# Attention scores as one fp32 product instead of three fp32r products, ten transpositions of the probabilities instead of twelve, and new orders on every engine

## The reference

```python
q = (einsum('bld,ed->ble', layernorm(x), Wq) + bq)      # 16 heads of 8
k, v = split(einsum('bmc,ec->bme', ctx, Wkv) + bkv)
att = softmax(einsum('blhd,bmhd->blmh', q, k) * scale, axis=2)
x = x + tanh(g_xattn) * (einsum('blmh,bmhd->blhd', att, v) @ Wo.T + bo)
cur = layernorm(x)
for r in range(4):                                       # 4 rounds, 4 experts, top 2
    cw = softmax over the two best of (cur @ Wg[r] + bg[r])
    cur = cur + sum_e cw[e] * (gelu(cur @ W1[e] + b1[e]) @ W2[e] + b2[e])
x = x + tanh(g_ffn) * cur
```

## Time and profile before

| | |
|---|---|
| median of 3 runs | 482.22 us (480.55 to 482.83) |
| the profiled execution | 479.67 us, of which its span, first to last instruction, is 477.9 us |
| busy in the span: TensorE, weight loads | 459.7 us (96%), 371.5 us (78%) |
| VectorE, ScalarE, GpSimd | 372.4 us (78%), 380.4 us (80%), 75.4 us (16%) |
| granted TensorE clock, mean | 0.995 of full speed |

### The profile page before, as it was taken

How to read it: one execution, slowest core, us unless ns; L and a number is a source line. 1 busy time by engine, 2 the same in 40 slices (tenths; PEclk the granted TensorE clock), 3 DMA queues, 4 the chain that set the end, 5 groups by cost and what they waited for, 6 DMA issues and landing times.

```text
span 477.9 us, 9057 instructions
## 1 busy us (share of the span) xinstructions
PE 459.7 (96%) x2969; PEld 371.5 (78%) x2969; DVE 372.4 (78%) x749; ACT 380.4 (80%) x781; POOL 75.4 (16%) x116
## 2 busy tenths in 40 slices
PE   6788999999999999999999999999999999999997
PEld 5566778878888788888888888888888888888885
DVE  4789889889796968876877787779767876887776
ACT  2587898878695987887888698869887988798773
POOL 4484898432200000000000000000000000000000
PEclk9899999999999999999999999999999999999999
DMA  5490000022002200300040004000400030023001
GB/s 138 132 253 15 1 17 16 2 91 89 2 0 90 86 3 1 139 40 1 1 178 1 1 1 178 0 2 2 176 1 0 23 158 1 1 78 123 22 2 45
DMA packets 15173, 25.21 MB, mean 53 GB/s; under 512 B 3505, under 2 KB 11542, under 8 KB 13078
## 3 DMA queue, kind: packets, MB, share of 16 engines
q1 hardware_dynamic: 11152, 22.05, 13.1%
q0 software_dynamic: 2592, 2.10, 2.6%
q10 hardware_dynamic: 1382, 0.49, 0.4%
HBM read 22.82 MB, written 1.18 MB: 50 GB/s over the span
## 4 chain that ended last, share of the span: by engine, by line
PE 86%; DVE 6%; ACT 3%; issue 3%; DMA 1%; SPq 1%; DVEq 0%; ACTq 0%
PE ps L1420 12%; PE ps L1407 12%; PE ps L1422 12%; PE ps L1421 12%; PE ps L1409 12%; PE ps L1408 12%; PE ps L1299 2%; PE ps L1318 2%; PE ps L1323 2%; PE ps L1284 1%; DMA gates<-in_g_ffn_dram 1%; DVE rT_sb L942 1%; ACT prob L716 1%; DVE least L918 1%; ACT probT L725 1%
## 5 line engine op out<-in xcount | busy, mean ns | idle before, releaser
L977 DVE TENSOR_TENSOR h_lo<-g_sb,h_hi 128x512 fp32r<-128x512 f32 x256 | 170.0, 688 | 75.6 <-ACT h_hi L829 75.4
L822 ACT ACTIVATE g_sb<-ps,cols 128x512 f32<-128x512 f32 x256 | 174.7, 694 | 35.6 <-PE ps L1409 34.1
L829 ACT ACTIVATE h_hi<-g_sb 128x512 fp32r<-128x512 f32 x256 | 156.0, 641 | 0.0
L1420 PE MATMUL ps<-h_hi,w_hi 128*128 128x512 f32 x252 | 101.6, 403 | 0.0
L1407 PE MATMUL ps<-x_hi,w_hi 128*128 128x512 f32 x256 | 101.1, 395 | 0.0
L1409 PE MATMUL ps<-x_hi,w_lo 128*128 128x512 f32 x256 | 100.1, 391 | 0.0
L1408 PE MATMUL ps<-x_lo,w_hi 128*128 128x512 f32 x256 | 99.8, 390 | 0.0
L1422 PE MATMUL ps<-h_hi,w_lo 128*128 128x512 f32 x252 | 99.6, 395 | 0.0
L1421 PE MATMUL ps<-h_lo,w_hi 128*128 128x512 f32 x252 | 99.5, 395 | 0.0
L1409 PEld LDWEIGHTS ps<-x_hi,w_lo 128*128 128x128 f32 x256 | 48.0, 188 | 11.3
L1408 PEld LDWEIGHTS ps<-x_lo,w_hi 128*128 128x128 f32 x256 | 48.1, 188 | 10.8
(11 more groups left out here) (153 smaller groups left out, 470.9 us busy)
## 6 DMA issues: line engine op xcount, KB each, us to landing
cwb_even<-cw_rows SPq DMA_DIRECT2D x8, 1024.0 KB, 5.3
cwb_odd<-cw_rows SPq DMA_DIRECT2D x8, 1024.0 KB, 4.9
w_hi<-in_L_ffn_W_dram POOLq DMA_DIRECT2D x2, 1024.0 KB, 8.2
x_sb<-in_x_dram SPq DMA_DIRECT2D x4, 256.0 KB, 5.9
w_in<-in_L_ffn_W_dram SPq DMA_DIRECT2D x1, 1024.0 KB, 6.0
out_dram<-xn SPq DMA_DIRECT2D x3, 256.0 KB, 2.3
ctx_sb<-in_ctx_dram ACTq DMA_DIRECT2D x4, 115.5 KB
v_st<-v_sb SPq DMA_DIRECT2D x8, 38.5 KB
```

The lines of the kernel that those rows point to most:

```text
L822: nc.scalar.activation(g_sb[:, k, :], ps[:, k, :], ACT.Gelu_apprx_tanh, bias=b1_c[:, e * NF + k:e * NF + k + 1]).then_inc(gelu_done, 1)
L829: nc.scalar.activation(h_hi[:, u % 2, k, :], g_sb[:, k, :], ACT.Copy).then_inc(hi_done, 1)
L977: nc.vector.tensor_tensor(h_lo[:, u % 2, k, :], g_sb[:, k, :], h_hi[:, u % 2, k, :].bitcast(F32), ALU.subtract).then_inc(lo_done, 1)
L1420: mm(yb, w2_hi[:, w], hh, start=k == 0, stop=False)
```

## The change

1. **Scores.** `q_hi`, `q_lo`, `k_hi`, `k_lo` and all work that splits q and k are gone. `scores` multiplies `q_st` by `k_st`, both fp32, one matmul for each head group.
2. **Blocks.** Two head groups (616 rows of probabilities) are now cut together into five blocks of 128, 128, 128, 128 and 104 rows, ten blocks a batch. The transposition groups hold 4, 4 and 2 blocks (`GROUPS`). `v_st` and `row_head` get a further index z for the group's place in its pair, and the list `pieces` gets as long as there are cuts.
3. **Orders.** Other orders in the start (input transfers, transpositions, warm-up matmuls, the tanh of the gates) and in the slots (tables and the order inside a slot, on all engines).

```diff
+    for z in range(NZ):
+        for j in range(HQ):
+            at, end = (HQ * z + j) * M, (HQ * z + j + 1) * M
...
+                pieces.append((z, j, k - 2 * z, at - P * k, stop - P * k, at - first, stop - first))
...
-            passes = ((q_hi, k_hi), (q_hi, k_lo), (q_lo, k_hi))
...
-                for n, (qs, ks) in enumerate(passes):
-                    for q in range(NQ):
-                        rows = slice(32 * q, 32 * q + 32)
-                        t = mm(ps[:, SC + q, 0:HM], qs[rows, c % 2, at], ks[rows, b % 2, :],
-                               start=n == 0, stop=n == len(passes) - 1)
+                for q in range(NQ):
+                    rows = slice(32 * q, 32 * q + 32)
+                    t = mm(ps[:, SC + q, 0:HM], q_st[rows, c % 2, at], k_st[rows, b % 2, :], start=True, stop=True)
                 t.then_inc(scores_done, 1)
...
-                for k in range(PG):
-                    q, c = (PG * g + k) // KC, (PG * g + k) % KC
-                    n, at = rows_of[c], q * HM + RP * c
-                    t = tr(bank(key)[0:n, k * L:(k + 1) * L], prob[:, b % 2, at:at + n], ident[:, :])
+                for k in range(GROUPS[g], GROUPS[g + 1]):
+                    n, at = rows_of[k % BLOCKS], k // BLOCKS * HP + k % BLOCKS * P
...
-        CTX_AT = {4: 2, 6: 3}
-        K_AT = {1: 1, 4: 2, 8: 3}
+        CTX_AT = {2: 2, 7: 3}
+        K_AT = {0: 1, 4: 2, 8: 3}
         V_AT = {3: 1, 7: 2, 10: 3}
-        LK_AT = {2: 1, 6: 2, 10: 3}
...
-        LOW_AT = {2: 1, 5: 2, 9: 3}
         W_LAG = 1
-        PT_DVE = {0: 2, 6: 1}
+        GROUPS = (0, 4, 8, 10)
+        PT_DVE = {2: 0}
...
-                for j, k, row, row_end, m, m_end in pieces:
-                    sp.dma_start(v_st[row:row_end, c % 2, k, DH * j:DH * (j + 1), :],
-                                 v_sb[m:m_end, c, DH * j:DH * (j + 1), :]).then_inc(v_ld[c], 16)
+                for z, j, k, row, row_end, m, m_end in pieces:
+                    sp.dma_start(v_st[row:row_end, c % 2, k, z, DH * j:DH * (j + 1), :],
+                                 v_sb[m:m_end, c, z, DH * j:DH * (j + 1), :]).then_inc(v_ld[c], 16)
...
-            act.wait_ge(gates_ld, 32)
-            nc.scalar.activation(tgates[:, :], gates[:, :], ACT.Tanh).then_inc(tg_ready, 1)
             move_k(0)
...
+            exponentials(0, 1)
+            stage_q("b")
             act.wait_ge(gates_ld, 32)
             nc.scalar.activation(tgates[:, :], gates[:, :], ACT.Tanh).then_inc(tg_ready, 1)
```

More of the change, by code:

```diff
@@ L59, in flamingo_gated_block @@
     KC = 3
-    RP = -(-HM // KC)
-    rows_of = [min(RP, HM - RP * c) for c in range(KC)]
-    pieces = []
[L63 to L71, removed]
+    NZ = 2
+    PAIRS = NQ // NZ
+    HP = NZ * HM
+    BLOCKS = -(-HP // P)
+    rows_of = [min(P, HP - P * k) for k in range(BLOCKS)]
+    assert BLOCKS == 5 and HM <= P * KC
+    pieces = []
+    for z in range(NZ):
+        for j in range(HQ):
+            at, end = (HQ * z + j) * M, (HQ * z + j + 1) * M
+            first = at
+            while at < end:
+                k = at // P
+                stop = min(end, P * (k + 1))
+                assert 0 <= k - 2 * z < KC
+                pieces.append((z, j, k - 2 * z, at - P * k, stop - P * k, at - first, stop - first))
+                at = stop
     with ExitStack() as stack:
@@ L160, in flamingo_gated_block @@
         kT = early("kT", [P, B * M])
[L161 to L164, removed]
+        q_st = early("q_st", [P, 2, CH])
         shifted = early("shifted", [P, 2, HM])
-        k_hi = early("k_hi", [P, 2, HM], F32R)
-        k_lo = early("k_lo", [P, 2, HM], F32R)
+        k_st = early("k_st", [P, 2, HM])
         prob = early("prob", [P, 2, NQ * HM])
@@ new lines, in expert_order @@
+            def expert_order():
+                nc.gpsimd.memset(lgs[:, :, :], 0.0).then_inc(zero_done, 1)
+                nc.gpsimd.memset(wg_w[:, :, :, :].bitcast(F32), 0.0).then_inc(zero_done, 1)
+                nc.gpsimd.memset(before[:, :, :], 1.0).then_inc(order_step, 1)
+                nc.gpsimd.memset(after[:, :, :], 1.0).then_inc(order_step, 1)
+                pool.wait_ge(order_step, 2)
+                nc.gpsimd.affine_select(out=before[:, :, :], in_=before[:, :, :], compare_op=ALU.is_ge, fill=0.0,
+                                        base=-1, pattern=[[1, E], [-1, E]], channel_multiplier=0).then_inc(order_ready, 1)
+                nc.gpsimd.affine_select(out=after[:, :, :], in_=after[:, :, :], compare_op=ALU.is_ge, fill=0.0,
+                                        base=-1, pattern=[[-1, E], [1, E]], channel_multiplier=0).then_inc(order_ready, 1)
@@ L700, in stage_q @@
                     act.wait_ge(scores_done, TC * (c - 1))
-                nc.scalar.activation(q_hi[:, g, at], bank(("Q", c))[:, at], ACT.Identity,
-                                     bias=bq_s[:, 0:1]).then_inc(q_hi_done, 1)
+                nc.scalar.activation(q_st[:, g, at], bank(("Q", c))[:, at], ACT.Identity,
+                                     bias=bq_s[:, 0:1]).then_inc(job_act, 1)
             def exponentials(b, half):
@@ L1133, in _ @@
                     smallest(b + 1, 1)
+                if b >= 3:
+                    add_residual(b - 3)
                 if b + 1 < B:
                     smallest(b + 1, 0)
+                if b == WEIGHTS0_SLOT:
+                    weights(0)
+                if b in PT_DVE:
+                    copy_pt(b, PT_DVE[b])
+                if b in MOMENTS:
+                    moments(*MOMENTS[b])
+                if b + 1 < B:
+                    shift(b + 1)
+                if b == ROUTER0_SLOT:
+                    router(0)
+                if b in NORMALISE:
+                    normalise(NORMALISE[b])
+                if b == ROUTER1_SLOT:
+                    router(1)
+                if b in SPLIT_X:
+                    split_x(SPLIT_X[b])
                 if b == 3:
```

325 lines of the change are left out of this document (143 added, 182 removed).

## The result

| | before | after |
|---|---|---|
| median of 6 runs | 481.51 us (479.74 to 482.83) | 475.69 us (474.77 to 478.36) |
| the profiled execution | 479.67 us, span 477.9 us | 478.16 us, span 476.4 us, clock 0.992 |

The ratio of after to before is 0.9902, 95% interval 0.9875 to 0.9929, which is 4.7 us less (3.4 to 6.0). Ratios here leave out four executions far above the others of their kernel, one each of before_fp32 and v_early_experts_later and two of before_twelve_pieces. Three of after's executions took 474.8 to 475.0 us at a granted clock of 1.000, three took 476.4 to 478.4 us at 0.992 to 0.996; the profile is of the second kind. A second profile of the same kernel (the last experiment) is of the first kind, 475.00 us with a span of 473.3 us.

What follows compares the result with a forecast made beforehand. The expert stage was taken as fixed, TensorE-bound, and loop slots as set by a circle through three engines. Start -1.7, slots -1.7, -0.1 and -1.45, late values +2.1 and +0.2 gave -2.65 us: median 479.6 us, range 474.5 to 485.

Steps and rivals of the forecast that it cites:

- A: Whole kernel, as summed: late values give back half of the gain; -1 to -4.5 us; chance 0.42.
- B: Whole kernel: values not late, or the loop packs better; 472 to 477.6 us; chance 0.26.
- Scores: Score product on TensorE: four fp32 row tiles overlap, 0.52 us in all, +0.12 us a batch.
- Rival D: Score product: fp32 row tiles don't overlap, 6 to 12.5 us on top, 486 to 492 us; chance 0.13.
- By the rule the scores would cost a third more: Score product: the skill's four passes for true fp32 against three fp32r passes, a third more cost.
- Values: SyncE's twelve pieces take 9.4 us, values there 10.2 to 10.6 us after the copy; stalls +2.1 and +0.2 us.
- Slots with q: Slots 2, 5, 9: VectorE's q_lo and its wait fall out; sum -1.7 us.
- Slots 3 and 4: Router's weights move behind everything: slot 3 6.83 to 5.2, slot 4 5.08 to 6.6 us; sum -0.1 us.
- But VectorE then begins slot 4 2.6 us late: Slot 4: the router's weights delay VectorE's start by 2.6 us, so the slot takes 6.6 us, from 5.08.
- Slot 5: Slot 5: 5.91 to 5.1 us without q_lo; values' lead 10.2 us, a stall of 0 to 0.35, taken as 0.2.
- The start: Before the second scores: tanh moves behind, splits of k and q go; second scores near 18.2 us, -1.7 us.
- Slots 10 to 15: End of the loop: only a little transposition work is lost; -0.5 us.

Runs made afterwards that it cites:

- before_fp32: The kernel before with q and k in fp32, one product and no low parts or splits; blocks and orders as before: 479.13 us, ratio 0.996.
- v_early_experts_later: v_early with GpSimd's two 1 MB expert-weight transfers one slot later and the splitting of these weights in slots 5 to 12: ratio 0.9877.
- before_twelve_pieces: The kernel before with each of the six transfers that place the values issued as two, each with half of the columns: ratio 1.0024.
- the last experiment: The changed kernel run once more without any edit, for a profile at full clock: 475.00 us.
- twelve_blocks: The changed kernel with twelve blocks of 102 or 103 rows and six value transfers again; fp32 scores and new orders stay: 474.03 us, ratio 0.987.
- three_pass: The changed kernel with the fp32 score product replaced by three fp32r passes over the high parts, low parts left out: 477.39 us, ratio 0.9922.
- before_twelve_pieces_again: The kernel before with its six value transfers issued as twelve, run once more for a profile at full clock: 479.58 us.
- v_early: The changed kernel with the values made in slots 1, 6 and 10 in place of 3, 7 and 10: 473.73 us, ratio 0.9855.
- v_early_one_warm: v_early with one warm-up product instead of six ahead of the first scores: 475.59 us, ratio 0.9881.
- router_weights_slot6: The changed kernel with the split of the router's weights in slot 6 in place of slot 3: 476.26 us, one run.
- experts_wait: v_early_one_warm with GpSimd issuing the 1 MB w2_hi transfer only once all twelve pieces of the first values have landed: 475.64 us, ratio 0.9879.

## Why the prediction was right, and where not

The forecast was 479.6 us and -2.65 us; measured were 475.69 us and about -4.7 us by the ratio. The sign and the range hold; the size is 2 us off. Of the rivals, A's mechanism came true, values that are late and give back part of the gain, but not its number: -4.7 us is more than its -4.5, and 475.69 us lies outside its 477.7 to 481.2 and inside B's 472 to 477.6. B's first half, values that are not late, is false; its second, a loop that packs better, is true in part. That the sum of so many terms, some of them far off, stayed within the range is in part luck: slots 3 to 5 came out 2.1 us low and 2.1 us high against their terms. Term by term, with the second profile of after (full clock), in us against before's profile:

| term | forecast | measured |
|---|---|---|
| start | -1.7 | 16.59 - 19.94 = -3.35 |
| slots 0 and 1 | -0.1 | 9.00 - 8.81 = +0.2 |
| slot 2 | -0.75 | -0.8 |
| slots 3 and 4 | -0.1 | 9.73 - 11.91 = -2.2 |
| slot 5, late values included | -0.6 | 7.40 - 5.91 = +1.5 |
| slot 6 | -0.6 | -0.5 |
| slots 7 and 8 | -0.25 | 9.92 - 10.33 = -0.4 |
| slot 9, late values included | +1.95 | 7.28 - 5.05 = +2.2 |
| slots 10 to 15 | -0.5 | -1.3 |
| sum | -2.65 | -4.65 |

The three parts can be told apart by four profiles, which differ by one part each: before, before_fp32 (part 1), twelve_blocks (parts 1 and 3), after's second profile (all). The loop takes 83.28, 83.31, 81.15 and 81.96 us, the start 19.94, 17.01, 16.61 and 16.59. So the fp32 scores gave the start, the new orders gave the loop, and the ten blocks took 0.8 us back.

**Scores.** Right: fp32 row tiles overlap, 0.80 us for the block instead of 0.70 (forecast +0.12). Rival D is out, and three_pass shows that the form of the product hardly matters. "By the rule the scores would cost a third more": the block costs a seventh more, and nothing in the total.

**Values.** Right: 9.3 to 9.45 us for twelve pieces, 10.6 us from the end of the copy to first use in slot 5 (37.57 to 48.21 in the first profile) and in before_twelve_pieces_again, 10.7 us in slot 9 of the second profile, forecast 10.2 to 10.6. In slot 9 of the first profile it was 10.0 and 11.3 us. Rival B's first half is out.

**Slots with q** were mis-sized, which the late values hide in the table. For q_lo's end I had booked 0.8 us in slot 5. But with the values in time that slot took 5.72 us in v_early and 6.01 in twelve_blocks, against 5.91 before and my 5.1; in before_fp32, the edit alone, it took 6.0. Only slot 2 paid.

**Slots 3 and 4: the step that failed** is "But VectorE then begins slot 4 2.6 us late". I took the 2.5 us of the router's weights for what they cost anywhere. Alone they take 0.75 us; the rest was waiting for GpSimd, which split the expert weights and spread k at that time. Slot 3 came out as forecast, 5.22 us, slot 4 at 4.51 instead of 6.6.

**Slot 5** failed with it: "the lead is slot 4 and 3.6 us of slot 5, 10.2 us". With slot 4 2.1 us shorter the lead is 8.1 us, and the values, ready by the clock of SyncE's queue and not by the slots, held slot 5. What slot 4 gained, slot 5 paid: together they take 11.9 us in both profiles, and 6.6 + 5.3 = 11.9 by my terms. By accident so, in part: under the wait for the values VectorE's held normalisation lies hidden, and no run took away the one without the other.

**The start** was mis-sized, -1.7 for -3.35 us; 1.4 us of the difference is there only where after keeps its clock (the first profile, with its clock at half for 3.4 us of the start, has -2.0). Before too had its clock at half for 3.4 us, the 0.91 of the earlier trace rows, of which my sum said nothing. **Slots 10 to 15** were mis-sized too: slots 14 and 15 take 9.58 us instead of 10.51, where before's VectorE did the second reduction ahead of a residual for which TensorE waited 0.78 us; I had not costed that order. That the other orders gave this was read from the two traces, not tested alone.

## What to carry to other kernels

Price a transfer queue by its number of transfers before changing how data is cut: the new cut saved 2.8 us over the loop and cost 3.6 in the two slots where values came late, and starting them earlier won 1.6 back. Before booking an operation at its profiled time, look what GpSimd does in the same microseconds: a price with a wait in it does not move with the operation. And where a start gets faster, list every transfer that it releases earlier, and what small transfers are still on the way.

## What the runs showed of the hardware that I had not expected

**VectorE held by GpSimd.** An operation that touches only SBUF and takes 0.16 to 0.23 us alone took 0.41 to 0.78 us in before (two of them in the earlier trace rows) when it met one of GpSimd's, and ended with it. Four normalising operations took 1.11 us beside an idle GpSimd (v_early, from 42.13 us) and 2.25 and 2.90 us in the two profiles of after, beside its splitting. The Trainium skill ("SBUF — State Buffer", SBUF: two separate sides) says that the two engines share a port pair, and that one instruction of either can hold it by an exclusive lock until it ends. The trace agrees, by the ends of the operations above.

**A large transfer holds up small ones.** The product with the values followed the end of the last piece's issue by 1.24 to 1.28 us where no large transfer ran (67.22 to 68.45, 46.96 to 48.21, 70.40 to 71.68 us), and by 4.8 us beside the 1 MB transfer of GpSimd's queue (21.31 to 26.07 in v_early_one_warm), 3.5 us in router_weights_slot6 (21.45 to 24.99) and 3.7 in three_pass (21.17 to 24.85). The Trainium skill ("DMA: Bandwidth & Descriptors", Queues, rings and completion order) says that a transfer engine takes turns between its queues, a packet at a time. The trace has records of both queues from 22 to 23.5 us, 27 of the pieces' to some 900 of w2_hi's; whether turns explain so small a share was not tested.

**The clock after a short idle time.** Granted clock at half, 1.2 GHz instead of 2.4, for 3.4 us: in slot 9 of after's first profile, 0.6 us before 2.8 us of idle time ended, in experts_wait 1.8 us behind one of 1.55 us; in after's second profile and in v_early idle times of 2.2 and 1.55 us were followed by full clock. In slot 9 the fall cost 1.25 us on top of the idle time, and whether the clock falls was not the same from run to run.
